# Weight preparation of a macaron transformer block: row blocks quantised in pairs, with two quantised buffers and loads released one buffer earlier

## The reference, cut to what matters

```
x = x + 0.5 * ffn(layernorm(x))
x = x + attn(layernorm(x))
x = x + 0.5 * ffn(layernorm(x))

def fp4_quant_dequant(x):            # blocks of 16 along the last dim
    scale = max(max|xb| / 6.0, 1e-12)
    q = _GRID[searchsorted(_MID, |xb / scale|)] * sign(xb) * scale
def fp4_linear(x, w):  einsum('bsk,nk->bsn', quant(x), quant(w))
def ffn(x):  fp4_linear(silu(fp4_linear(x, w_gate)) * fp4_linear(x, w_up), w_down)
```

## Time and profile before

| | us |
|---|---|
| median of the two timed runs | 6336.4 |
| the two timed runs | 6309.7 and 6363.1 |
| profiled execution, its own time | 6290.45 |
| span of its slowest core (core 0) | 6288.9 |
| spans of the 8 cores | 6257.9 to 6288.9 |

### The profile page before, as it was taken

One profiled execution on the slowest core, in us unless ns is written; L12 is line 12 of the kernel. 1 busy time (PEld: TensorE's weight loads), 2 busy tenths in 40 slices (PEclk: granted clock), 3 DMA queues, 4 the chain that ended last, 5 costly groups with the idle time before them and its releaser, 6 DMA issues.

```text
span 6288.9 us, 36730 instructions; the slowest of 8 cores (6257.9 to 6288.9 us)
## 1 busy us (share of the span) xinstructions
PE 1863.1 (30%) x9264; PEld 926.8 (15%) x9264; DVE 2561.3 (41%) x3706; ACT 1647.0 (26%) x1718; POOL 363.0 (6%) x605
## 2 busy tenths in 40 slices
PE   0000000023343333442333333333333333333333
PEld 0000000012111111111221111111111111111111
DVE  5666663045344453442221322222245535355352
ACT  1111112332122221224334324323412222122221
POOL 2322332000000000000000000000000000000000
PEclk9999999996666666665555555555556666766767
DMA  3111112320210202101010110111010121201212
GB/s 112 51 49 52 52 55 68 110 68 24 61 50 25 63 24 60 51 25 62 27 54 14 54 41 14 54 40 46 22 41 27 31 61 43 60 27 30 62 42 87
DMA packets 210009, 304.64 MB, mean 48 GB/s; under 512 B 30160, under 2 KB 128464, under 8 KB 208784
## 3 DMA queue, kind: packets, MB, share of 16 engines
q1 hardware_dynamic: 184896, 256.98, 13.3%
q0 software_dynamic: 24912, 45.32, 2.0%
HBM read 268.11 MB, written 34.08 MB: 48 GB/s over the span
## 4 chain that ended last, share of the span: by engine, by line
DVE 37%; PE 26%; ACT 15%; issue 10%; DMA 9%; DVEq 1%; POOL 1%; ACTq 0%; SPq 0%; POOLq 0%
ACT L137 10%; PE psg L505 5%; PE psu L508 5%; PE psA L727 4%; DVE q_cF L137 4%; DMA wdb<-s_wdT 3%; PE psd L598 3%; DVE hb L137 3%; DVE q_iF L137 3%; DVE q_rF L137 3%; DVE q_bmF L137 2%; DVE wkD L137 2%; DVE q_cW L137 2%; DVE btB L137 2%; DVE q_ivF L137 2%
## 5 line engine op out<-in xcount | busy, mean ns | idle before, releaser
L137 ACT ACT_TABLE_LOAD x815 | 1045.6, 1283 | 4536.0 <-PE pstB L553 1042.5
L505 PE MATMUL psg<-wgb,xq 128*128 128x512 bf16 (+1 forms) x1536 | 574.1, 382 | 39.3 <-ACT xq L137 21.7
L508 PE MATMUL psu<-wub,xq 128*128 128x512 bf16 (+1 forms) x1536 | 571.1, 380 | 0.0
L553 PE MATMUL pstB<-identb,btB 128*128 128x128 bf16 x704 | 90.3, 306 | 1158.4 <-DVE btB L137 1158.4
L137 DVE TENSOR_TENSOR hb<-wkA,psu 128x512 f32<-128x512 f32 (+1 forms) x192 | 123.5, 643 | 677.3 <-ACT wkA L137 677.3
L598 PE MATMUL psd<-wdb,hq 128*128 128x512 bf16 x1408 | 353.4, 400 | 115.7 <-DMA wdb<-s_wdT 93.5
L315 PE MATMUL psW<-identb,wqb 128*128 128x128 bf16 x528 | 67.1, 306 | 974.0 <-DVE wqb L137 843.1
L137 DVE TENSOR_TENSOR btB<-qs_b,cosr 128x256 bf16<-128x256 bf16 x128 | 37.5, 293 | 735.1 <-ACT qp_b L137 735.1
L727 PE MATMUL psA<-xn_fm,wbufA 128*128 128x256 bf16 x1024 | 238.8, 413 | 276.8 <-ACT qp_b L137 254.4
L445 PE MATMUL pstA<-identb,btA 128*128 128x128 bf16 x256 | 32.4, 307 | 918.1 <-DVE btA L137 918.1
L1118 POOL DMA_DIRECT2D out<-R x16 | 8.4, 535 | 4978.4 <-DVE R L137 4978.4
(11 more groups left out here) (128 smaller groups left out, 3757.3 us busy)
## 6 DMA issues: line engine op xcount, KB each, us to landing
wdb<-s_wdT SPq DMA_DIRECT2D x176, 256.0 KB, 2.6
wgb<-s_wgT SPq DMA_DIRECT2D x320, 128.0 KB, 2.8
wub<-s_wuT SPq DMA_DIRECT2D x320, 128.0 KB, 2.9
wbufA<-s_wq SPq DMA_DIRECT2D x64, 256.0 KB, 5.6
wbufA<-s_wk SPq DMA_DIRECT2D x64, 256.0 KB, 6.8
wbufA<-s_wv SPq DMA_DIRECT2D x64, 256.0 KB, 4.1
wbufA<-s_wo SPq DMA_DIRECT2D x64, 256.0 KB, 4.3
R<-x POOLq DMA_DIRECT2D x16, 512.0 KB, 14.5
```

Of the source, the lines that this page charges most:

```text
L137: instr = f(*a, **kw)
L505: t_.matmul(psg[:, pp * 512: pp * 512 + mw], lhs, wgbuf[:, wp * 4096 + k * 512: wp * 4096 + k * 512 + mw], start=(k == 0), stop=(k == DK - 1))
L508: last = t_.matmul(psu[:, pp * 512: pp * 512 + mw], lhs, wubuf[:, wp * 4096 + k * 512: wp * 4096 + k * 512 + mw], start=(k == 0), stop=(k ...
L553: last = t_.transpose(pstB[:, qpp * 1024 + sb * 128: qpp * 1024 + (sb + 1) * 128], btB[:, qpp * DM + sb * 128: qpp * DM + (sb + 1) * 128], ...
```

## The change

The w_gate and w_up chunks are taken two at a time: one load of 256 rows into the two halves of a buffer, one quantisation of width 2048, and two groups of 8 transposes. w_down keeps its chunks of 128 rows. `wqb` becomes two buffers, used in turn. The load no longer waits for all VectorE work, but for the quantisation that last used its own load buffer; the quantisation no longer waits for all transposes, but for those that last read its own half of `wqb`. The destinations of the stores are computed from the pair. The index that picks the buffer and the half of `wqb` restarts at 0 with every weight matrix.

```
         wldA = WSB("wldA", [128, FFI], F32)
         wldB = WSB("wldB", [128, FFI], F32)
-        wqb = WSB("wqb", [128, FFI], BF16)
+        wqb = WSB("wqb", [128, 2 * FFI], BF16)
...
-            for name, dsrc, ddstT, nchunk, F in [
-                ("wg", dwgate, s_wgT, NKI, DM),
-                ("wu", dwup, s_wuT, NKI, DM),
-                ("wd", dwdown, s_wdT, DK, FFI),
+            for name, dsrc, ddstT, nchunk, F, PR in [
+                ("wg", dwgate, s_wgT, NKI, DM, 2),
+                ("wu", dwup, s_wuT, NKI, DM, 2),
+                ("wd", dwdown, s_wdT, DK, FFI, 1),
             ]:
...
-                for j in range(nchunk):
-                    buf = wldA if (j % 2 == 0) else wldB
-                    slot = slw[j % 2]
+                items = [(j0, min(PR, nchunk - j0))
+                         for j0 in range(0, nchunk, PR)]
+                for ii, (j0, pr) in enumerate(items):
+                    buf = wldA if (ii % 2 == 0) else wldB
+                    W = F * pr
+                    slot = slw[ii % 2]
...
-                        y.wait_ge(sdv.h, sdv.n)
-                        y.dma_start(out=buf[:, 0:F],
-                                    in_=dsrc[j * 128:(j + 1) * 128, 0:F]).then_inc(slot.h, 16)
+                        prev = ld_rd.get(id(buf))
+                        if prev:
+                            y.wait_ge(sdv.h, prev)
+                        y.dma_start(
+                            out=buf[:, 0:W].rearrange("p (t c) -> p t c", c=F),
+                            in_=dsrc[j0 * 128:(j0 + pr) * 128, 0:F]
+                            .rearrange("(t p) c -> p t c", p=128)).then_inc(slot.h, 16)
...
                         v.wait_ge(slot.h, ldm)
-                        v.wait_ge(spe.h, spe.n)
-                        sdv.inc(quantW(v, buf[:, 0:F], F, wqb[:, 0:F]))
+                        prev = wqb_rd.get(qb)
+                        if prev:
+                            v.wait_ge(spe.h, prev)
+                        sdv.inc(quantW(v, buf[:, 0:W], W, wqb[:, qb * FFI: qb * FFI + W]))
                     V(_)
                     qm = sdv.n
-                    nsb = F // 128
+                    ld_rd[id(buf)] = qm
+                    nsb = W // 128
...
                         T(_)
                         tm = spe.n
+                        wqb_rd[qb] = tm
```

More of the change, by code:

```diff
@@ L279, in build_program, with _ @@
         with nc.psum_tensor("psW", [128, 2048], BF16) as psW:
-            for name, dsrc, ddstT, nchunk, F in [
-                ("wg", dwgate, s_wgT, NKI, DM),
-                ("wu", dwup, s_wuT, NKI, DM),
-                ("wd", dwdown, s_wdT, DK, FFI),
+            ld_rd = {}
+            wqb_rd = {}
+            ppx = [0]
+            for name, dsrc, ddstT, nchunk, F, PR in [
+                ("wg", dwgate, s_wgT, NKI, DM, 2),
+                ("wu", dwup, s_wuT, NKI, DM, 2),
+                ("wd", dwdown, s_wdT, DK, FFI, 1),
             ]:
                 sst = sgw if name in ("wg", "wu") else sgwd
-                for j in range(nchunk):
-                    buf = wldA if (j % 2 == 0) else wldB
-                    slot = slw[j % 2]
-                    def _(y, j=j, buf=buf, dsrc=dsrc, F=F):
-                        y.wait_ge(sdv.h, sdv.n)
-                        y.dma_start(out=buf[:, 0:F],
-                                    in_=dsrc[j * 128:(j + 1) * 128, 0:F]).then_inc(slot.h, 16)
+                items = [(j0, min(PR, nchunk - j0))
+                         for j0 in range(0, nchunk, PR)]
+                for ii, (j0, pr) in enumerate(items):
+                    buf = wldA if (ii % 2 == 0) else wldB
+                    bk = (name, ii % 2)
+                    W = F * pr
+                    slot = slw[ii % 2]
+                    def _(y, j0=j0, pr=pr, buf=buf, dsrc=dsrc, F=F, W=W):
+                        prev = ld_rd.get(id(buf))
[5 more added lines that the diff above has]
+                            .rearrange("(t p) c -> p t c", p=128)).then_inc(slot.h, 16)
                     Y(_)
@@ L296, in build_program, with _ @@
                     ldm = slot.n
-                    def _(v, buf=buf, F=F, ldm=ldm, slot=slot):
+                    qb = ii % 2
+                    def _(v, buf=buf, W=W, ldm=ldm, slot=slot, qb=qb):
                         v.wait_ge(slot.h, ldm)
-                        v.wait_ge(spe.h, spe.n)
-                        sdv.inc(quantW(v, buf[:, 0:F], F, wqb[:, 0:F]))
+                        prev = wqb_rd.get(qb)
+                        if prev:
+                            v.wait_ge(spe.h, prev)
+                        sdv.inc(quantW(v, buf[:, 0:W], W, wqb[:, qb * FFI: qb * FFI + W]))
                     V(_)
                     qm = sdv.n
-                    nsb = F // 128
+                    ld_rd[id(buf)] = qm
+                    nsb = W // 128
                     for g0 in range(0, nsb, 8):
                         gn = min(8, nsb - g0)
-                        pp = ((g0 // 8) + j) % 2
-                        def _(t, g0=g0, gn=gn, pp=pp, qm=qm):
+                        pp = ppx[0] % 2
+                        ppx[0] += 1
+                        jcol = j0 + (g0 * 128) // F
+                        c0 = (g0 * 128) % F
+                        def _(t, g0=g0, gn=gn, pp=pp, qm=qm, qb=qb):
                             t.wait_ge(sdv.h, qm)
@@ L316, in _ @@
                                     psW[:, pp * 1024 + s * 128: pp * 1024 + (s + 1) * 128],
-                                    wqb[:, (g0 + s) * 128:(g0 + s + 1) * 128],
+                                    wqb[:, qb * FFI + (g0 + s) * 128: qb * FFI + (g0 + s + 1) * 128],
                                     identb[:])
@@ L329, in build_program, with _ @@
                         am = sac.n
-                        def _(g, j=j, g0=g0, gn=gn, pp=pp, am=am, ddstT=ddstT,
-                              sst=sst):
+                        def _(g, jcol=jcol, c0=c0, g0=g0, gn=gn, pp=pp, am=am,
+                              ddstT=ddstT, sst=sst):
                             g.wait_ge(sac.h, am)
@@ L335, in _ @@
                                 g.dma_start(
-                                    out=ddstT[(g0 + s) * 128:(g0 + s + 1) * 128,
-                                              j * 128:(j + 1) * 128],
+                                    out=ddstT[c0 + s * 128: c0 + (s + 1) * 128,
+                                              jcol * 128:(jcol + 1) * 128],
                                     in_=evacW[:, pp * 1024 + s * 128: pp * 1024 + (s + 1) * 128],
```

## The result

| | before | after |
|---|---|---|
| median of the timed runs, us | 6296.3 (10 runs) | 5977.3 (11 runs) |
| ratio after/before | | 0.9509, 95% interval 0.9475 to 0.9542 |
| span of the slowest core in the profiled execution, us | 6288.9 | 5999.6 |
| from the start to the last copy out of `psW`, us | 1048.3 | 736.6 |

The change makes the kernel 4.9% faster. The same cut by stretch as in the earlier trace rows, of the kernel after on its slowest core, core 6; the columns are those of the earlier trace rows.

What follows compares the result with a forecast made beforehand. VectorE was taken to bound the changed preparation; 252.4 us saved up to w_down's start plus 95.5 in w_down, 348 together, off a level of 6321 gave 5973 us, range 5910 to 6060.

Steps and rivals of the forecast that it cites:

- The round of a pair: In w_gate and w_up, VectorE sets a pair's time: 19.5 us of quantisation plus gaps and stalls, 19.8 us.
- The start: Before the third pair: 6.6 us from extra loads and 3.5 us for transposes move its start from 48.4 to 58.5 us.
- The chain's length: In w_gate and w_up, copies, stores and landings take 16.8 to 21.6 us a pair; taken as 19.2, just under VectorE's 19.8.
- the room: Slack of the copy and store sequence beside VectorE's 19.8 us a pair: 3.0 us, from 16.8 us undisturbed.
- The matrix changes: At w_gate to w_up and w_up to w_down, VectorE waits for load and transposes: 10 us each, 20 together.
- w_down: VectorE sets the w_down chunk at 25.7 us, 8 x 25.7 = 205.6; with the end, 226.0 instead of 321.5 us.
- The tail: From the last w_down quantisation's end to the last copy's end: 20.4 us, as in the kernel before.
- The held stores: Six of nine full-width VectorE instructions hold GpSimd's stores; at full cost 4.8 us a pair, half of the stretches hit.
- first rival: In the weight preparation, copies, stores and landings set the pace: 6057 us at full cost, 6015 at half; chance 0.18.
- Starvation: In the weight preparation, each of nine full-width VectorE instructions lets one store through: 544 us slower, 6865 us; chance 0.03.
- the exposed load: In w_gate and w_up, loads still come only after the last quantisation, adding 5.4 us a pair: 6092 us; chance 0.04.
- The rest unchanged: Attention weights and the FFN calls behind keep every instruction and TensorE its clock: a term of 0.

Runs made afterwards that it cites:

- pairs-only: The changed kernel with both old waits put back (loads for all VectorE work, quantisations for all transposes): 6142.5 us, 0.9768 of the kernel before.
- buffers-only: The changed kernel with both new waits and two halves of wqb, but w_gate and w_up in single chunks of 128 rows: 6056.6 us, 0.9616 of before.
- own-halves: The changed kernel with separate store semaphores, so a copy waits only for stores of its half of evacW: 5914.7 us, 0.9405 of before.
- its repeat: The changed kernel, unaltered, run again on the chip of the follow-up runs: 5991.1 us, 0.9512 of the kernel before.
- running index: The changed kernel with one buffer index running on through the three matrices instead of restarting: 5968.1 us, 0.9484 of the kernel before.

## Why the prediction was right, and where it was off

The mechanism held: the two waits left VectorE's path, the round of a pair became VectorE's own time, and the pairs-only and buffers-only runs bear it out. That the time came so near, 5977.3 for 5973, is luck. Two misses of opposite sign meet in it. The level of the kernel before was 6296, not the 6321 that I took from three runs: 25 us too high. The preparation gave 312 us, not 348: 36 us too much. Together they make 5984; the last 7 us lie within the spread of the timed runs (5967.6 to 6008.2). By its own steps:

- *The round of a pair, 19.8 us:* right. 19.71 us in the rows above, 19.6 us of them the quantisation. The straight line in the width (19.5) was good to 0.1 us. The 20 pairs took 399.8 us (495.2 - 58.4, less 37.0 for the matrix changes) for 396: 5 us of it are waits of VectorE for TensorE in three rounds of w_gate, 2.4, 1.3 and 1.3 us.
- *The load hidden:* right, and the pairs-only and buffers-only runs show it. What I hadn't said is that the transposes' wait was as long as the load's.
- *The start, 58.5 us:* right, 58.4. The first ScalarE work was released 6.4 us later than before, for 6.6 forecast from 2.1 MB more at 316 GB/s.
- *The chain's length, 19.2 us a pair:* too short, and this is the step that failed. From the third pair of w_gate to the ninth the copies come every 10.00 us, 20.0 us a pair. That is over VectorE's 19.7, where I had it 0.6 us under. The sum had two additions to the undisturbed 8.39 us a group: 1.2 us for held stores, and nothing for landings beside a load, which I had left to "the room". Read from the timelines of ScalarE and GpSimd over these groups, the issue of eight stores takes 5.31 us for 4.25 undisturbed, 1.06 more, and the time from the last issue to the next copy's table load is 1.85 us for 1.30, 0.55 more. The held stores were sized about right; the missing term is the landings. Of the 15 times in the whole preparation that a copy was kept waiting for a landing for more than 1.6 us after the last issue, 13 had a load of 1 or 1.4 MB in flight when the last store went out; of the 49 other times that a landing released it, 7. So late landings go with a load in flight, and the new waits send each load out beside the stores of some group.
- *The matrix changes, 10 us each and at most 14:* wrong, 20.9 and 16.1, 17 us in all, by that step. I had "behind up to one store round". But the chain came out of the start about a round and a half behind, and at 20.0 us against 19.7 it had nothing to catch up with, so its lag of 30 us stayed all through w_gate; it could not grow further, because VectorE then waited for its half of `wqb`, the three waits above. The own-halves run takes the lag away, and the waits with it.
- *w_down, 8 x 25.7:* right, 207.4 us from the first block maximum to the last quantisation's end for 205.6.
- *The tail, 20.4 us as before:* wrong by the same step, 34.0; 13.6 us. With 17.0, 3.8, 1.8 and -0.1 from above this makes up the 36.1 us, and it is why the last copy ended at 736.6 and not near 700.
- *The held stores:* the hold is there, but I gave it one instruction too many. I had six of the nine full-width instructions hold GpSimd, the TENSOR_TENSOR on bfloat16 among them. Of the changed kernel's 528 stores 74 took over 0.7 us, and each of the 74 ended 0.12 or 0.13 us after the end of a full-width TENSOR_SCALAR. The stores that began within such an instruction and over 0.6 us before its end were all held, 65 of them, while the 18 that began in the same way within the bfloat16 TENSOR_TENSOR took 541 ns at most, though it is as fast. So it is five of nine, and at full cost 4.0 us a pair instead of 4.8. One group of stores beside it, from w_down:

```profile
593.30 1.63 DVE L137 TENSOR_TENSOR q_rW<-q_rW,q_cW 128x2816 bf16<-128x2816 bf16 x1
593.45 4.25 POOL L354 DMA_DIRECT2D s_wdT<-evacW  x8 [4.14 <-ACT evacW L137]
595.03 3.09 DVE L137 TENSOR_TENSOR wqb<-q_rW,q_shW 128x2816 bf16<-128x2816 bf16 x1
```

  In the mean over each matrix a store's issue is 633 to 675 ns for 541:

```profile
L354 POOL DMA_DIRECT2D s_wuT<-evacW x176 | 117.4, 675 | 119.2 <-ACT evacW L137 113.6 <-issue 5.6
L354 POOL DMA_DIRECT2D s_wdT<-evacW x176 | 114.9, 660 | 113.3 <-ACT evacW L137 110.5 <-issue 2.8
L354 POOL DMA_DIRECT2D s_wgT<-evacW x176 | 110.1, 633 | 150.1 <-ACT evacW L137 146.8 <-issue 3.3
```

- *The rivals:* the chain of stores set the pace in few rounds, 5 us in w_gate and 1.5 in w_down, but its mechanism was there and took 31 us more at the changes and the end; forecast and first rival were two sides of one thing, not alternatives. Starvation and the exposed load did not occur.
- *The rest unchanged:* right for the instructions; on core 0 the first FFN call took what it took before, 1570.2 us for 1570.4. On the slowest core, at a granted clock of 0.68, it took 26 us more; I had given the clock 0.

## What to carry to other kernels

Taking a wait off the bounding engine is worth what the next wait leaves: here, in w_gate and w_up, the load's and the transposes' came within 0.1 us of each other. When a second chain is nearly as long as the new round, add to it what the change itself puts beside it (here a load in flight beside the stores' landings), and ask not only whether it fits but how far it lags at the start and in how many rounds it can catch up; the lag is paid at every place where the two must meet. And where waits at such meeting places look like a bug of their own, free the lagging chain first: the index across the matrices gave next to nothing before and its full 14 us after.

## What the runs showed of the hardware that I had not expected

- A 32 KB store's landing stretched from 1.7 to 7.0 us when two 1 MB loads went out together, and such a landing holds this kernel's whole chain, since the next copy waits for all eight stores. In the median w_gate's stores still landed in 1.7 us; one late landing in a group is enough.
- Beside VectorE's full-width TENSOR_SCALARs GpSimd's issue of a store waited for the instruction's end and 0.12 us more; beside the TENSOR_TENSOR on bfloat16, which takes the same 1.23 us at width 2048, it did not. Over five profiles (before, changed, its repeat, running index, own halves) an issue was caught by an instruction that began up to 0.227 us after it, and none by one that began 0.228 us or more after.
- Issued from ScalarE's queue, a 32 KB store took 0.45 us in the median and never over 0.74 us in w_gate, beside the same VectorE instructions that stretched GpSimd's to 1.50 us.
